# Experts and routing of a four-block network: three orders of work changed

## The chip, the cores and the metric

The kernel runs on one core of one Trainium2 chip. The metric is the device time of one execution in microseconds (us). A core has five engines with instruction streams of their own, which meet only at semaphores: TensorE (matrix products and transposes, called PE in the rows), VectorE (DVE), ScalarE (ACT), GpSimd (POOL) and SyncE (SP), which here only starts transfers and clears semaphores. GpSimd starts the indexed transfers, gathers and scatters.

## The reference, cut to what matters

Four conditioned blocks run one after the other on `x` of 16 x 256 tokens with 256 features. The change lies in the second half of the last one, a mixture of eight experts, each of which chooses its own 512 of the 4096 tokens:

```python
tok = x.reshape(-1, d)                       # 4096 x 256
gate = softmax(tok @ Wgate.T)                # 4096 x 8
vals, idx = jax.lax.top_k(gate.T, k_cap)     # each expert its 512 tokens
g = _ln(tok[idx_flat], mlp_g, mlp_b)         # gathered, normalised
y = gelu(einsum('ked,ehd->keh', g, fc1s) + b1s, approximate=True)
y = einsum('keh,edh->ked', y, fc2s) + b2s
tok = tok.at[idx_flat].add(y * w[..., None]) # scattered back, added
```

## The kernel before, in words

The program is a row of blocks; at the border of a block all engines meet. Attention and MLP blocks fill the first 3126 us. Behind them stand two that the change touches.

`route` (L2465 and on). TensorE turns the 4096 tokens in eight groups of 512 (`transposes`, bank tiles `r_bank`, two sets of two), VectorE evicts the first half `k = 0` of groups 0 to 3 to `r_xt` and ScalarE all other halves; TensorE may write group 2 only when group 0 is evicted on both. Then follow logits, a softmax on VectorE in two halves, a search for each expert's 512th largest gate in 15 rounds of VectorE and TensorE, and the lists of tokens, which become `idx`. VectorE works in the order of the code: constants, a wait for four small loads (`const_in`), four conversions (L2674 to L2677), the evictions (L2681), 14 shifts that fill `r_bits` (L2684), the softmax. At the same time ScalarE rounds the first expert's `moe_w1` to its high part and GpSimd subtracts that from it (L2535), the low part. Last, GpSimd gathers the first expert's tokens in four pieces of 128 into `xg`, all on one semaphore `first_in`.

`experts` (L2807 and on). Each expert has 512 tokens in four tiles (`SC` = 4), features in two halves (`KD` = 2) and a hidden width of 1024 in eight parts (`MC` = 8). Every product is made of three in fp32r with high and low parts (`three`, L2935 to L2937), so every operand is split: ScalarE copies the high part, VectorE subtracts it. In the body of expert e:

- TensorE makes the up products of e, the down products of m = 0 and 1, the transposes of the normalised tokens of e + 1 (`moe_tp`, L2943), and the down products of m = 2 to 7.
- ScalarE makes the gelu and high part of `moe_h` for m = 0 to 7, then the high parts of `moe_xt` and of both weights `moe_w` of e + 1.
- VectorE makes the low parts of `moe_h`; behind m = 2 the statistics of the gathered tokens of e + 1 up to `moe_ve` (`normalise`); behind m = 3 `moe_xn` (`centre`, L2993), for which it needs the root; behind m = 7 `moe_xm` (gain and offset, L3002), the low parts of `moe_xt` and of the up weights; then y (L3032), y2, that is y times the gate (L3038), and the low part of the down weights.
- GpSimd waits for the scatters of e - 1, releases the y2 buffer, makes the reciprocal root `moe_rstd` for e + 1 (`token_rstd`, L2865), copies the indices of the scatter, waits for `moe_xn` of e + 1, gathers the tokens of e + 2, waits for y2 of e and issues its four scatters (L2881).

GpSimd's semaphore waits that other engines' work must not overtake are followed by an increment of their own (`gated_wait`). The root can start when VectorE has written `moe_ve`. Before the loop, the first expert goes through `normalise(0)`, `centre(0)`, `transposes(0)`, `modulate(0)` and `x_hi(0)` as whole steps, each waiting for the whole of the last.

## Time and profile before

| | us |
|---|---|
| median of three runs | 3471.63 |
| lowest, highest | 3470.23, 3478.52 |
| profiled execution | 3478.18 |
| its span, first to last instruction | 3476.4 |
| TensorE busy in the span | 3109.7 (89%) |
| VectorE busy | 2206.5 (63%) |
| ScalarE busy | 1693.4 (49%) |
| GpSimd busy | 807.6 (23%) |
| mean granted clock of TensorE | 0.952 |

Times in the rows are microseconds from the start of the span. A timeline row gives the start, the busy time (of all that are merged in the row, x4 for four), the engine, the line of the kernel, the operation with its result and its sources, and in brackets how long the engine was idle before it and what ended that. The granted clock is TensorE's: 1.00 is 2.4 GHz, 0.50 is 1.2 GHz, and a value between is a mean over the stretch. The ends of matrix products are modelled, so that one reaches beyond the start of the next.

### The profile page before, as it was taken

The page shows a single profiled execution, that of the slowest core. Times are in us where ns is not written, and L with a number is a line of the kernel's source. Part 1 is how long each engine was busy: PE and PEld are TensorE (multiplying, and loading weights), DVE is VectorE, ACT ScalarE, POOL GpSimd, SP SyncE. Part 2 cuts the span into 40 slices and gives each one's busy share as a digit, 9 for nine tenths or more (in the row PEclk, how much of TensorE's full clock was granted, in tenths as well). Part 3 has the DMA queues.
Part 4 walks back from the last instruction along what each step waited for, and adds up shares of the span by engine and source line. Part 5 has one row for each costly group of instructions (what it writes and reads, how often), then busy time and mean ns, then how long its engine had stood idle before and what let it go on. Part 6 is the DMA issues. An engine that isn't in the chain of part 4 may idle for free. (4 is left out here: it accounts for less than half of the span.)

```text
span 3476.4 us, 71011 instructions
## 1 busy us (share of the span) xinstructions
PE 3109.7 (89%) x26346; PEld 2545.5 (73%) x26346; DVE 2206.5 (63%) x4254; ACT 1693.4 (49%) x3084; POOL 807.6 (23%) x656
## 2 busy tenths in 40 slices
PE   7899999997998969999999698799999999982786
PEld 5777877786898959877777587576767676762676
DVE  4566656574666766567777467565656565758564
ACT  3344434443554435545454354565656566651453
POOL 1221112211112321112222111322222222221443
PEclk8999999999999989999999899899999999995898
DMA  4000000000100010100000100000000000003442
GB/s 158 10 6 6 4 5 6 6 6 16 36 19 20 0 46 0 49 1 0 0 0 0 56 24 19 28 1 0 0 0 0 0 0 0 0 14 112 114 114 52
DMA packets 64656, 80.66 MB, mean 23 GB/s; under 512 B 9666, under 2 KB 56514, under 8 KB 64308
## 3 DMA queue, kind: packets, MB, share of 16 engines
q1 hardware_dynamic: 58436, 71.13, 6.7%
q0 software_dynamic: 6144, 8.52, 1.3%
q8 instruction: 46, 0.75, 0.1%
q14 instruction: 30, 0.25, 0.0%
HBM read 66.80 MB, written 12.85 MB: 23 GB/s over the span
## 5 line engine op out<-in xcount | busy, mean ns | idle before, releaser
L915 POOL TENSOR_TENSOR L0a_prob<-L0a_prob 128x1024 f32<-128x1024 f32 x48 | 117.3, 2444 | 570.7 <-PE L0a_o L1270 570.7
L1017 ACT ACTIVATE L0a_prob<-L0a_st 128x512 f32<-128x512 f32 x256 | 138.7, 597 | 201.7 <-PE L0a_st L1237 175.0
L921 POOL TENSOR_TENSOR L3a_shift<-L3a_neg,L3a_mx 128x256 fp32r<-128x256 f32 x128 | 95.7, 748 | 554.5 <-DVE L3a_mx L1496 552.4
L1017 ACT ACTIVATE L3a_prob<-L3a_st 128x512 f32<-128x512 f32 x256 | 138.8, 597 | 128.5 <-PE L3a_st L1237 128.5
L1496 DVE TENSOR_REDUCE L0a_mx<-L0a_s 128x2 f32<-128x512 f32 x256 | 164.4, 683 | 39.2 <-PE L0a_s L1213 37.3
L1845 ACT ACTIVATE L2a_prob<-L2a_st 128x512 f32<-128x512 f32 x256 | 132.2, 604 | 116.3 <-PE L2a_st L1876 116.3
L1486 DVE SCALAR_TENSOR_TENSOR L3a_qk_lo<-raw,cols_sb,L3a_qk_hi 128x256 fp32r<-128x256 f32 x256 | 156.4, 650 | 36.5 <-ACT L3a_qk_hi L1008 36.5
L1496 DVE TENSOR_REDUCE L3a_mx<-L3a_s 128x2 f32<-128x512 f32 x256 | 163.8, 679 | 18.2 <-PE L3a_s L1213 18.1
L2108 DVE TENSOR_REDUCE L2a_mx<-L2a_s 128x2 fp32r<-128x512 f32 x256 | 163.5, 681 | 14.5 <-PE L2a_s L1876 14.5
L1435 DVE RECIPROCAL L0a_rsum<-L0a_sum 128x256 f32<-128x256 f32 x16 | 28.1, 1758 | 197.8 <-PE L0a_sum L1285 176.2
L1435 DVE RECIPROCAL L3a_rsum<-L3a_sum 128x256 f32<-128x256 f32 x16 | 28.1, 1758 | 174.4 <-PE L3a_sum L1285 155.3
L1475 DVE TENSOR_TENSOR L0a_qk_lo<-L0a_st,L0a_qk_hi 128x512 fp32r<-128x512 f32 x128 | 86.8, 687 | 69.9 <-ACT L0a_qk_hi L977 69.8
L915 POOL TENSOR_TENSOR L3a_prob<-L3a_prob 128x1024 f32<-128x1024 f32 x48 | 117.6, 2451 | 52.7 <-PE L3a_o L1270 51.1
L1270 PE MATMUL L3a_o<-L3a_prob,L3a_v 128*64 128x256 f32 x1024 | 124.6, 385 | 0.0
L1270 PE MATMUL L0a_o<-L0a_prob,L0a_v 128*64 128x256 f32 x1024 | 124.6, 385 | 0.0
L972 ACT ACTIVATE L0a_o_hi<-L0a_o 128x512 fp32r<-128x512 f32 x64 | 40.5, 632 | 129.1 <-PE L0a_o L1107 64.7
L1270 PEld LDWEIGHTS L3a_o<-L3a_prob,L3a_v 128*64 128x64 f32 x1024 | 67.8, 136 | 40.8 <-issue 6.6
L1270 PEld LDWEIGHTS L0a_o<-L0a_prob,L0a_v 128*64 128x64 f32 x1024 | 67.8, 136 | 40.7 <-issue 6.6
L990 ACT ACTIVATE L3a_prob<-L3a_st 128x512 f32<-128x512 f32 x128 | 77.2, 603 | 33.9 <-PE L3a_sum L1168 33.9
L1449 DVE TENSOR_TENSOR L3a_o<-raw,L3a_s 128x512 f32<-128x512 f32 x64 | 43.9, 686 | 75.8 <-PE L3a_s L1126 75.8
L1105 PE MATMUL L0a_st<-L0a_xt,L0a_wq 128*128 128x256 f32 x256 | 77.6, 303 | 15.1 <-POOL L0a_wo L909 10.0
L1105 PE MATMUL L3a_st<-L3a_xt,L3a_wq 128*128 128x256 f32 x256 | 77.9, 304 | 11.5 <-POOL L3a_wo L909 8.9
(605 smaller groups left out, 11528.4 us busy)
## 6 DMA issues: line engine op xcount, KB each, us to landing
raw<-in_moe_w SPq DMA_DIRECT2D x16, 1024.0 KB, 6.0
x_sb<-in_x SPq DMA_DIRECT2D x1, 4096.0 KB, 24.5
L0a_gate<-gate_rows SPq DMA_DIRECT2D x32, 128.0 KB, 3.8
L0m_gate<-gate_rows SPq DMA_DIRECT2D x32, 128.0 KB, 3.8
L2a_gates<-gate_rows SPq DMA_DIRECT2D x2, 2048.0 KB, 10.0
L2m_gate<-gate_rows SPq DMA_DIRECT2D x32, 128.0 KB, 3.7
out_x<-x_sb SPq DMA_DIRECT2D x1, 4096.0 KB, 18.0
token_rows<-x_sb SPq DMA_DIRECT2D x1, 4096.0 KB, 29.8
```

The source lines that it names most:

```text
L915: nc.gpsimd.tensor_tensor(both[:, :, :, 0:N], both[:, :, :, 0:N], both[:, :, :, N:2 * N], ALU.add).then_inc(halves_done, 1)
L921: nc.gpsimd.tensor_tensor(shift[:, u % 4, :, :, :], neg64[:].unsqueeze(1).unsqueeze(1).to_broadcast([P, 2, TT, 64]), mx[:, u % 2, :, :].un ...
L990: A(sq[:, c % 4, :], qk_bank(c)[:], ACT.Square).then_inc(sq_done, 1)
L1017: A(prob[:, u % 4, h, :], st_ps[u % 2][h][:], ACT.Exp, scale=64 ** -0.5).then_inc(p_done, 1)
L1105: mm(out, lhs[0], rhs[0], start=start, stop=False, skip_group_check=True)
L1270: last = mm(o_ps[rows(h), (u % 2) * N:(u % 2 + 1) * N], v[:, kt, hd * 64:(hd + 1) * 64], prob[:, u % 4, h, kt * N:(kt + 1) * N], start=(kt ...
L1435: V.reciprocal(rsum[:], sum_ps[:, 0:N]).then_inc(rsum_done, 1)
L1475: V.tensor_tensor(qk_lo[:, c, :], qk_bank(c)[:], qk_hi[:, c, :].bitcast(F32), ALU.subtract).then_inc(qklo_done, 1)
L1486: ins = V.scalar_tensor_tensor(qk_lo[:, u, at], raw[:, u, at], col(name), qk_hi[:, u, at].bitcast(F32), ALU.add, ALU.subtract)
L1496: V.tensor_reduce(mx[:, u % 2, h, :], s_ps[h][:].rearrange("p (t n) -> p t n", t=TT), AX.X, ALU.max).then_inc(mx_done, 1)
L1845: A(prob[:, 2 * (w % 2) + h, :], st_ps[w % 2][h][:], ACT.Exp, scale=0.25).then_inc(p_done, 1)
L2108: V.tensor_reduce(mx[:, w // 2 % 2, :, at], s_ps[h][:].rearrange("p (t n) -> p t n", t=TT), AX.X, ALU.max).then_inc(mx_done, 1)
```

## The change

It has three parts. In the body of each expert GpSimd makes the root of the next expert before it waits for the scatters of the last one, and before it releases y2. In the routing VectorE's wait for the constants and the four conversions stand behind the four evictions and the fourteen shifts. And the first expert is taken by pieces: a semaphore for each of the four gathers; statistics and mean of one tile after the other; `moe_xn` with a signal per tile, behind which TensorE makes that tile's two transposes; `moe_xm` and both parts of `moe_xt` by halves with a signal each. The copies of the gate weights go behind `moe_ve`, and seven more semaphores are in use.

```diff
--- before.py
+++ after.py
@@ -2541,7 +2541,7 @@
             pool.wait_ge(idx_ready, 1)
             for s in range(SC):
                 pool.indirect_dma_start(moe["xg"][:, s, :], None, t["token_rows"][:, :],
-                                        bass.IndirectOffsetOnAxis(ap=g["idx"][:, 0, s:s + 1], axis=0)).then_inc(moe["first_in"], 16)
+                                        bass.IndirectOffsetOnAxis(ap=g["idx"][:, 0, s:s + 1], axis=0)).then_inc(moe["first_in"][s], 16)
 
         @block.scalar
         def _(act):
@@ -2670,11 +2670,6 @@
             V.memset(thr[:], 0).then_inc(ready, 1)
             step(V.tensor_reduce(same[:], g["ident"][:].rearrange("p (t e) -> p e t", e=E), AX.X, ALU.add))
             V.tensor_copy(same_b[:], same[:].unsqueeze(1).to_broadcast([P, HALF, E])).then_inc(ready, 1)
-            dve.wait_ge(const_in, 64)
-            V.tensor_copy(iota_h[:], iota_f[:, 0:LOW]).then_inc(ready, 1)
-            V.tensor_copy(tri_b[:], tri[:]).then_inc(ready, 1)
-            step(V.tensor_scalar(tok_f[:], tval[:], float(P), pval[:, 0:1], ALU.mult, ALU.add))
-            V.tensor_scalar(tok_h[:], tok_f[:], -2048.0, None, ALU.add).then_inc(ready, 1)
             READY = TRIES + 5
             for i in range(4):
                 dve.wait_ge(tp_done, KD * i + 1)
@@ -2682,6 +2677,11 @@
             dve.wait_ge(ready, TRIES + 1)
             for n in range(1, BITS // 2):
                 step(V.tensor_scalar(bits[:, n, :], bits[:, n - 1, :], 2, None, ALU.logical_shift_right))
+            dve.wait_ge(const_in, 64)
+            V.tensor_copy(iota_h[:], iota_f[:, 0:LOW]).then_inc(ready, 1)
+            V.tensor_copy(tri_b[:], tri[:]).then_inc(ready, 1)
+            step(V.tensor_scalar(tok_f[:], tval[:], float(P), pval[:, 0:1], ALU.mult, ALU.add))
+            V.tensor_scalar(tok_h[:], tok_f[:], -2048.0, None, ALU.add).then_inc(ready, 1)
 
             def softmax(h):
                 half = lambda a: a[:, HALF * h:HALF * (h + 1)]
@@ -2828,6 +2828,7 @@
         w1_in, w2_in, b2_in, w1_hi, w1_lo, w2_hi, w2_lo = (sem(x) for x in ("w1_in", "w2_in", "b2_in", "w1_hi", "w1_lo", "w2_hi", "w2_lo"))
         idx_done, gathered, scattered, weight_done, passed, passed_dve = (sem(x) for x in ("idx", "gathered", "scattered", "weight", "passed", "passed_dve"))
         idxo_done, weight_now, y2_free = sem("idxo"), sem("weight_now"), sem("y2_free")
+        first_xn, first_tp, first_xm, first_xhi = (sem(x) for x in ("first_xn", "first_tp", "first_xm", "first_xhi"))
         block = ctx.enter_context(nc.Block())
         w1_d = t["moe_w1"].rearrange("e (k p) n -> e p k n", p=P)
         w2_d = t["moe_w2"].rearrange("e (m p) n -> e p m n", p=P)
@@ -2865,11 +2866,11 @@
                 nc.gpsimd.tensor_tensor(rstd[:], ve[:], g["mhalf"][:, 0:SC], ALU.pow).then_inc(rstd_done, 1)
 
             def body(e, first, more, more2):
+                if more:
+                    token_rstd(e + 1)
                 if not first:
                     gated_wait(scattered, 16 * SC * e)
                 pool.sem_inc(y2_free, 1)
-                if more:
-                    token_rstd(e + 1)
                 nc.gpsimd.tensor_copy(idx_out[:], g["idx"][:, bass.ds(e, 1), :].squeeze(1)).then_inc(idxo_done, 1)
                 gated_wait(idxo_done, e + 1)
                 if more2:
@@ -2920,7 +2921,10 @@
 
             act.sem_inc(w1_hi, 1)
             act.sem_inc(w2_hi, 1)
-            x_hi(0)
+            for k in range(KD):
+                act.wait_ge(first_xm, k + 1)
+                nc.scalar.activation(xt[0][:, k, :], xm[:, k, :], ACT.Copy).then_inc(first_xhi, 1)
+            act.sem_inc(xhi_done, 1)
             body(0, True)
             with act.Fori(1, E - 1) as e:
                 body(e, True)
@@ -2965,7 +2969,13 @@
                         transposes(e + 1)
                 last.then_inc(down_done, 1)
 
-            transposes(0)
+            for s in range(SC):
+                pe.wait_ge(first_xn, s + 1)
+                for k in range(KD):
+                    last = nc.tensor.transpose(tp_ps[k][:, s * P:(s + 1) * P], xn[:, s, k * P:(k + 1) * P], g["ident"][:])
+                    if s == SC - 1:
+                        last.then_inc(first_tp, 1)
+            pe.sem_inc(tp_done, 1)
             with pe.Fori(0, E - 1) as e:
                 body(e, True)
             body(E - 1, False)
@@ -3043,10 +3053,31 @@
                     low(e + 1, w2_hi, w2, stage2, w2_lo)
 
             dve.sem_inc(down_free, 1)
-            normalise(0, moe["first_in"], 16 * SC)
-            centre(0)
-            modulate(0)
+            for s in range(SC):
+                dve.wait_ge(moe["first_in"][s], 16)
+                V.bn_stats(stats[:, s, :], xg[:, s, 0:D]).then_inc(stats_done, 1)
+                dve.wait_ge(stats_done, s + 1)
+                V.bn_aggr(mv[:, s, :], stats[:, s, :]).then_inc(aggr_done, 1)
+            dve.wait_ge(aggr_done, SC)
+            V.tensor_scalar(ve[:], mv[:, :, 1], 1e-5, None, ALU.add).then_inc(ve_done, 1)
+            V.tensor_copy(weight_next[:], xg[:, :, D:D + 1].squeeze(2)).then_inc(weight_done, 1)
             weights_now(0)
+            dve.wait_ge(rstd_done, 1)
+            for s in range(SC):
+                V.tensor_scalar(xn[:, s, :], xg[:, s, 0:D], mv[:, s, 0:1], rstd[:, s:s + 1], ALU.subtract, ALU.mult).then_inc(first_xn, 1)
+            dve.wait_ge(first_xn, SC)
+            dve.sem_inc(xn_done, 1)
+            gain, offset = COL_AT["L3_cond_mlp_g"], COL_AT["L3_cond_mlp_b"]
+            for k in range(KD):
+                dve.wait_ge(first_tp, k + 1)
+                V.tensor_scalar(xm[:, k, :], tp_ps[k][:], g["cols"][:, gain + k:gain + k + 1], g["cols"][:, offset + k:offset + k + 1],
+                                ALU.mult, ALU.add).then_inc(first_xm, 1)
+            dve.wait_ge(first_xm, KD)
+            dve.sem_inc(xm_done, 1)
+            for k in range(KD):
+                dve.wait_ge(first_xhi, k + 1)
+                ins = V.tensor_tensor(xt[1][:, k, :], xm[:, k, :], xt[0][:, k, :].bitcast(F32), ALU.subtract)
+            ins.then_inc(xlo_done, 1)
             low(0, w2_hi, w2, stage2, w2_lo)
             with dve.Fori(0, E - 1) as e:
                 body(e, True)
@@ -3089,7 +3120,7 @@
                "stage2": g["raw"][:, 4:8, :].rearrange("p c (m n) -> p (c m) n", n=D), "w1_in": g["first_w1_in"],
                "w1": [sb(f"moe_w1{j}", [P, KD, MLP], F32R) for j in range(2)],
                "w2": [sb(f"moe_w2{j}", [P, MC, D], F32R) for j in range(2)],
-               "idx_now": sb("moe_idx_now", [P, SC], U32), "xg": sb("moe_xg", [P, SC, ROW]), "first_in": sem("moe_first_in")}
+               "idx_now": sb("moe_idx_now", [P, SC], U32), "xg": sb("moe_xg", [P, SC, ROW]), "first_in": [sem(f"moe_first_in{s}") for s in range(SC)]}
         route(nc, t, g, out, moe)
         experts(nc, t, g, out, moe)
         with nc.Block() as block:
```

The listing of GpSimd's instructions shows the first part. This is the loop over the experts 1 to 5, before; `moe_rstd` is the root, `moe_xg` the gather, `out_x` the scatters, and the rows without a result are arithmetic on registers for the waits.

```order
L2890 ISA
L2852 REGISTER_ALU
L2865 TENSOR_TENSOR moe_rstd<-moe_ve,mhalf 128x4
L2873 ISA
L2873 COPY moe_idx_out<-idx_sb 128x4
L2852 REGISTER_ALU
L2857 ISA
L2857 COPY moe_idx_now<-idx_sb 128x4
L2860 DMA moe_xg<-token_rows,moe_idx_now 128x264 x4
L2881 DMA out_x<-moe_y,moe_idx_out 4096x256 x4
```

The same loop of GpSimd now:

```order
L2891 ISA
L2866 TENSOR_TENSOR moe_rstd<-moe_ve,mhalf 128x4
L2853 REGISTER_ALU
L2874 ISA
L2874 COPY moe_idx_out<-idx_sb 128x4
L2853 REGISTER_ALU
L2858 ISA
L2858 COPY moe_idx_now<-idx_sb 128x4
L2861 DMA moe_xg<-token_rows,moe_idx_now 128x264 x4
L2882 DMA out_x<-moe_y,moe_idx_out 4096x256 x4
```

The root stands first, before the register for the scatters' count is made; everything behind has its old order. The second part, on VectorE at the start of the routing, `-` before and `+` now:

```order
 L2671 TENSOR_REDUCE r_same<-ident_sb 128x8
 L2672 CAST r_same_b<-r_same 128x128
-L2674 CAST r_iota_h<-r_iota_f 128x32
-L2675 CAST r_tri_b<-r_tri 128x128
-L2676 TENSOR_SCALAR r_tok_f<-r_tval,r_pval 128x32
-L2677 TENSOR_SCALAR r_tok_h<-r_tok_f 128x32
-L2681 COPY r_xt<-r_bank 128x512 x4
-L2684 TENSOR_SCALAR r_bits<-r_bits 128x3 x14
+L2676 COPY r_xt<-r_bank 128x512 x4
+L2679 TENSOR_SCALAR r_bits<-r_bits 128x3 x14
```

The four evictions and the fourteen shifts are ahead of the four conversions, which follow there and are followed by the softmax as before.

## Rows read from the trace of the kernel before

**Rows 1.** Waits of GpSimd and TensorE, 2990 to 3480: total, times, longest us.
```profile
POOL moe_rstd L2865 <- DMA out_x<-moe_y,moe_idx_out: 20.6, 6, 3.6
...
PE moe_tp L2943 <- DVE moe_xn L2993: 22.8, 7, 9.2
```

**Rows 2.** Timeline of GpSimd, expert 1: start, us, operation, idle before.
```profile
3274.11 1.04 POOL L2865 TENSOR_TENSOR moe_rstd<-moe_ve,mhalf 128x4 f32<-128x4 f32 x1 [3.29 <-DMA out_x<-moe_y,moe_idx_out]
```

**Rows 3.** Timeline of VectorE, experts 0 to 6.
```profile
3258.74 1.42 DVE L3032 TENSOR_TENSOR moe_y<-moe_down,moe_b 128x256 f32<-128x256 f32 x4 [1.82 <-PE moe_down L2937]
...
3268.35 0.17 DVE L2988 TENSOR_SCALAR moe_ve<-moe_mv 128x4 f32<-128x4 f32 x1
...
3275.19 1.38 DVE L2993 TENSOR_SCALAR moe_xn<-moe_xg,moe_mv,moe_rstd 128x256 f32<-128x256 f32 x4 [6.04 <-POOL moe_rstd L2865]
...
3287.26 1.41 DVE L3032 TENSOR_TENSOR moe_y<-moe_down,moe_b 128x256 f32<-128x256 f32 x4
...
3432.58 1.42 DVE L3032 TENSOR_TENSOR moe_y<-moe_down,moe_b 128x256 f32<-128x256 f32 x4 [0.55 <-PE moe_down L2937]
```

**Rows 4.** Timeline of TensorE, experts 1 to 3.
```profile
3277.47 0.36 PE L2935 MATMUL moe_down<-moe_w,moe_h 128*128 128x256 f32 x1
...
3285.92 0.28 PE L2937 MATMUL moe_down<-moe_w,moe_h 128*128 128x256 f32 x1
...
3287.39 0.50 PE L2935 MATMUL moe_up<-moe_xt,moe_w 128*128 128x512 f32 x1 [1.19 <-DVE moe_w L3010]
...
3305.14 1.09 PE L2943 MATMUL moe_tp<-ident_sb,moe_xn 128*128 128x128 f32 x8 [2.06 <-DVE moe_xn L2993]
...
3316.08 0.40 PE L2935 MATMUL moe_up<-moe_xt,moe_w 128*128 128x512 f32 x1
```

**Rows 5.** Stretches: busy us of each engine, granted clock, DMA share, GB/s.
```profile
3272.00:3276.00 4.00, 2.57 (x22) 2.36 (x21) 0.81 (x3) 0.00 (x0) 1.20 (x2) 1.00 0.31 48
3306.00:3310.00 4.00, 4.00 (x24) 4.00 (x22) 2.48 (x5) 2.39 (x4) 2.83 (x3) 0.57 0.12 34
```

**Rows 6.** Timelines in the routing: GpSimd, ScalarE, VectorE, TensorE.
```profile
3128.68 4.48 POOL L2535 TENSOR_TENSOR moe_w<-raw,moe_w 128x2048 fp32r<-128x2048 f32 x1
...
3128.32 1.06 ACT L2553 ACTIVATE r_xt<-r_bank 128x512 f32<-128x512 f32 x2
...
3129.81 3.39 DVE L2674 CAST r_iota_h<-r_iota_f 128x32 f16<-128x32 f32 x1 [1.92 <-DMA r_tri<-in_tri]
...
3133.61 1.28 DVE L2681 COPY r_xt<-r_bank 128x512 f32<-128x512 f32 x2
...
3137.81 2.81 DVE L2684 TENSOR_SCALAR r_bits<-r_bits 128x3 uint32<-128x3 uint32 x14
...
3142.78 0.29 DVE L2690 COPY r_logit<-r_bank 128x128 f32<-128x128 f32 x1 [2.15 <-PE r_bank L2604]
...
3134.35 5.01 PE L2584 MATMUL r_bank<-ident_sb,x_sb 128*128 128x128 f32 x24 [5.88 <-DVE r_xt L2681]
...
3139.29 1.06 PE L2574 MATMUL r_bank<-r_xt,r_wide_wg 128*32 128x512 f32 x8
```

**Rows 7.** Timelines of GpSimd and VectorE, two earlier places.
```profile
46.52 2.50 POOL L900 TENSOR_TENSOR L0a_wv<-L0a_prob,L0a_wv 128x1024 fp32r<-128x1024 f32 x1 [8.30 <-ACT L0a_wv L1083]
...
47.81 1.25 DVE L1409 TENSOR_SCALAR L0a_ve<-L0a_mv 128x2 f32<-128x2 f32 x1
...
1085.61 0.98 POOL L386 TENSOR_TENSOR L1a_rstd<-L1a_ve,mhalf 128x2 f32<-128x2 f32 x1 [4.00 <-DVE L1a_ve L593]
...
1085.94 0.42 DVE L691 COPY L1a_v_row<-L1a_pt_ps 128x256 f32<-128x256 f32 x1
```

**Rows 8.** Timelines of VectorE and TensorE, first expert.
```profile
3221.59 0.17 DVE L2980 COPY moe_weight_next<-moe_xg 128x4 f32<-128x4 f32 x1 [4.31 <-PEq L2465]
...
3228.32 1.53 DVE L3002 TENSOR_SCALAR moe_xm<-moe_tp,cols_sb 128x512 f32<-128x512 f32 x2 [2.06 <-PE moe_tp L2943]
...
3232.34 0.76 PE L2935 MATMUL moe_up<-moe_xt,moe_w 128*128 128x512 f32 x1 [4.06 <-DVE moe_xt L3006]
```

## The prediction

> **What bounds the kernel now.** I read the waits first, over the last 486 us (the end of the attention, the routing and the experts), since everything that the diff touches lies there. Two rows stand out [rows 1]: GpSimd's reciprocal root `moe_rstd` waited 20.6 us in six waits for the scatters into `out_x` to land, and TensorE's transposes `moe_tp` waited 22.8 us in seven waits for VectorE's `moe_xn`, which needs that root. The six are the bodies of experts 1 to 6.
>
> The timelines of expert 1's body show one loop. GpSimd's root starts at 3274.11, after 3.29 us of waiting for the landing, so the last of the four scatters was issued by 3270.82 [rows 2]. VectorE had the root's input `moe_ve` at 3268.52, then sat idle 6.04 us until `moe_xn` at 3275.19 [rows 3]. From y to y an expert takes 28.52 us here (3258.74 to 3287.26), and (3432.58 - 3258.74) / 6 = 28.97 us on the mean of experts 0 to 6 [rows 3]. TensorE is full otherwise but not the only bound: it waits 2.06 us before the transposes of the next expert, and 1.19 us at 3287.39 for the low half of `moe_w` [rows 4], because the work behind the root (last `moe_h`, `moe_xm`, `moe_xt`, `moe_w`) came late as well. And in expert 2 the granted clock was 0.57 from 3306 to 3310 while in the same part of expert 1, 3272 to 3276, it was 1.00 [rows 5]: it fell behind the idle pieces of two experts in a row.
>
> In the routing, the chain is: transposes, evictions, logits, softmax on VectorE. VectorE's first conversion, 32 elements a row, took 3.39 us, from 3129.81 to 3133.20; GpSimd's subtraction for `moe_w` ran from 3128.68 to 3133.16. The first two evictions start behind it at 3133.61 and TensorE's third group of transposes waits 5.88 us for them [rows 6].
>
> **A: the root ahead of the wait for scatters.** Nothing is added or taken out; GpSimd's 1.04 us root moves ahead of a wait. It is queued behind the four scatter issues still, so it starts at 3270.8 plus 0.3 us, my estimate of the hand-over from the issue to the root: 3271.1 in place of 3274.1, a shift of 3.0 us. Its input is there since 3268.5. What is late next:
> - The chain through the root. From y to root: 3271.15 - 3258.74 = 12.4 us. From root to the next y: 3287.26 - 3274.11 = 13.15 us, unchanged, as all of it is serial behind the root on VectorE and ScalarE. Sum 25.5 us.
> - TensorE. From the first up product at 3287.39 to the transposes at 3305.14, less the 2.06 us, 15.7 us; transposes 0.9 of their 1.09, the rest being the drain; the rest of the down products at the full clock, 3277.47 to 3285.92 and one pitch of 0.12, 8.6 us [rows 4]. Sum 25.2 us, just under the chain's 25.5.
> So the period goes from 28.97 to 25.5 us, six times: 173.84 - 153.2 = **20.6 us**. It is more than six times 3.0 because the longer experts also lose their stretch at the low clock and their slower landings. What was moved past: the scatter wait now stands ahead of the index copies, the release of `y2` and the next gather. The gather's place was behind `moe_xn` anyway; the landing (3273.8, 0.3 before the old root) comes 0.2 us after the new end of `moe_xn` (3273.6), so the gather too starts almost 3 us earlier, and it is wanted only in the next expert. Low end for A: only TensorE's own wait goes, 6 x 2.06 = 12.4. High end: a period of TensorE's 25.2, 22.6.
>
> **B: conversions behind the first evictions.** In the new order VectorE goes to the evictions right after `same_b`. ScalarE's first eviction starts at 3128.32, two take 1.06 [rows 6], so the first is done at 3128.95, and TensorE's third group can start at 3129.0 in place of 3134.35. Three groups of 8 at the pitch of the full clock take some 2.9 us in place of 5.0, so the logits start at 3131.9 in place of 3139.29, and the softmax, 3.49 us behind them (3142.78 - 3139.29), could start at 3135.4. VectorE itself is later: evictions done at about 3131.2, then 14 shifts of `bits` (2.81 us [rows 6]), then four conversions (0.6 us without the stall). If the shifts are free of GpSimd's subtraction they end at 3134.0 and the conversions at 3134.6: softmax at 3135.4, 7.4 us gained. If they wait for its end at 3133.16, as the conversion did, the softmax starts at 3136.6: 6.1 gained. Here is what the rows give: a scalar operation of 2 elements, SBUF to SBUF, started at 47.81 beside GpSimd's product of 46.52 and took 1.25 us, where `moe_ve` of 4 elements takes 0.17 [rows 3], to 49.06, the product's end 49.02; a copy of 256 elements out of PSUM beside GpSimd's root at 1085.61 took its plain 0.42 [rows 7]. The shifts are of the first sort, the evictions of the second, so I take **6.1 us**. The searches behind are one chain and only move; GpSimd's first gather moves with its index; the row store's last wait was over long before. The low end is 0.4: the evictions stall too and start at 3133.2 in place of 3133.61.
>
> The Trainium skill, SBUF — State Buffer, "Who interferes with whom", says that a single-source VectorE operation within SBUF in a two-port mode and a GpSimd operation exclude each other for the whole instruction, and one with a PSUM source does not take part. The rows 6 and 7 agree to 0.04 us. By that rule the evictions are free and the shifts are held, which is the 6.1; without the rule for shifts it would be 7.4.
>
> **C: the first expert by pieces.** VectorE starts at 3221.59, and what it stood idle for in front of that was the block's border (PEq), not a gather [rows 8]: they have landed. So waiting per gather brings nothing. Statistics and means taken in turn cost four waits between them in place of one: some +0.3 us. Then `moe_xn` in four with a signal each: before, all 1.38 us of it [rows 3] came first and then all eight transposes, for which VectorE stood idle 2.06 us until 3228.32 [rows 8]; now TensorE starts behind the first quarter, 1.0 us earlier, less the 0.3. Then, before, both `moe_xm` (1.53), ScalarE's half, VectorE's half and the up products at 3232.34, 4.0 us behind 3228.32 [rows 8]. In halves: the first `moe_xm` starts one transpose (2.06 / 8, 0.26 us) before the last ends and takes 0.8, the second follows, ScalarE's halves lie beside it, VectorE's second half ends 0.6 after ScalarE's second: some 2.8 us. Sum -0.3 + 1.0 + 1.2 = **2.0 us** nearly exactly (3230.3 in place of 3232.3). Bounds: 0 (the semaphores eat it) to 2.5. The seven new semaphores are cleared at the end, 0.1 us or so: left out.
>
> **Sum.** 20.6 + 6.1 + 2.0 = 28.7 us off the profiled execution's own 3478.18 (span 3476.4): 3449.5. That execution was 6.55 above the median of the three runs, 3471.63; off the median it is 3442.9, which is the forecast.
>
> **Rivals.**
> - *The clock keeps falling.* For it: expert 2 had the fall, by the mean of 28.97 against expert 1's 28.52 others had it too (I take experts 2, 4 and 6), and TensorE still has short waits for `moe_h` in each expert. Against: the two longest idle pieces (2.06 and 1.19) go. Then every second expert has its transposes and the rest of its down products slow as now (3305.14 to 3316.08, 10.9 in place of 9.5 [rows 4]) and a period of 15.7 + 10.9 = 26.6: A is 173.84 - 3 x 25.53 - 3 x 26.6 = 17.4, sum 25.5, 3446.1. The Trainium skill, TensorE: Matmul & The Clock Gate, Part 1, has the clock released by activity and throttled after idleness; that speaks for the forecast, rows 5 agree with the direction.
> - *The evictions stall beside GpSimd.* B is 0.4, sum 23.0, 3448.6. Rows 7's copy out of PSUM is against it.
> - *Something else takes the root's place.* GpSimd is in line again with gather and scatters, or a transfer of weights arrives late since the loads, scatters and gathers now come closer; then only TensorE's own wait is saved: 12.4 + 6.1 + 2.0 = 20.5, 3451.1. For it: loads, gathers and scatters of an expert share 29 us today and 25.5 then. Against: no transfer holds anyone in rows 1 but the scatters that root.
> - *Slower.* The tighter loop leaves TensorE at 1.2 GHz through whole experts, as it was in the routing. An expert's up and down products are some 22 us at the full clock (13 or more of the 15.7, and the 8.6) and as much again at half; from 28.7 us of work done at half the clock, 1.3 experts, the change costs time. At two and a half: 3471.6 + 55 - 28.7 = 3498. Nothing in rows 5 has the clock fall while TensorE is full; it is here because all of A leans on the clock.
> - *It doesn't do what it says:* no, the order of GpSimd's row changes in the loop as the listing shows.
>
> **Chances.** Forecast 0.62 (its own range 3439 to 3447), clock 0.13, evictions 0.08, other bound 0.12, no visible change 0.03, slower 0.02. The range 3437 to 3457 takes in A's and B's ends but one (both lows together, 3458). About 0.3%, 10.4 us, can be told from no change: every case but the last two saves 20 us or more, so faster 0.95, same 0.03, slower 0.02.
>
> **What would show it.** A: root starts 0.3 us behind the last scatter issue, no wait for landings in front of it; y to y near 25.5 for experts 1 to 6; transposes wait under 0.3 us; clock 1.00 from 3240 on. B: third group of transposes some 2.5 us behind the first, shifts beside GpSimd's subtraction with the first stretched to its end, softmax 6 us sooner after the routing's start. C: up products 8.7 us behind the block's border in place of 10.8. It is wrong if a period stays above 27 us, or if the routing (its start to the first gather) is less than 4 us shorter.

## The result, and the profile after

The changed kernel takes 3439.34 us in the median of five runs (3433.54 to 3446.91), the kernel before 3471.63 in the median of five beside them (3463.62 to 3478.52): a ratio of 0.9905, 95% interval 0.9891 to 0.9919. The forecast was 3442.9 us (range 3437 to 3457), on the side of faster with 0.95.

The profiled execution took 3443.93 us with a span of 3442.1, against a span of 3476.4 before. Of these 34.3 us, 4.4 are no part of the change: the routing starts at 3122.18 where before it started at 3126.56, and nothing in front of it was touched. From the routing's start to the end the changed kernel takes 319.9 us and the kernel before 349.8: **29.9 us less, where the sum of the prediction was 28.7**. Split at rows that both traces have (us; `r_gate_t` VectorE's copy of the transposed gates, "border" is VectorE's first row of the experts, "up" TensorE's first up product, y0 to y7 VectorE's `moe_y` of the eight experts):

| stretch | before | after | only A | only B | only C |
|---|---|---|---|---|---|
| routing's start to `r_gate_t` | 29.46 | 23.19 | 29.44 | 23.15 | 29.48 |
| `r_gate_t` to border | 65.57 | 65.62 | 65.63 | 65.65 | 65.55 |
| border to up | 10.75 | 9.07 | 10.75 | 10.74 | 9.08 |
| up to y0 | 26.40 | 25.75 | 26.26 | 26.12 | 25.60 |
| y0 to y6 (six experts) | 173.84 | 152.36 | 151.66 | 174.25 | 174.45 |
| y6 to y7 | 23.50 | 23.53 | 23.49 | 23.52 | 23.50 |

So B is 6.3 us, C 1.7 (up to the first up product), A 21.5. Another 0.65 us lie between up and y0, in the first expert; whether C made them is taken up below.

The waits of the changed kernel from y0 to y6 (total, times, longest us), for [rows 1]:

```profile
DVE moe_xn L3003 <- POOL moe_rstd L2866: 16.8, 6, 2.8
...
POOL moe_idx_out L2874 <- DMA out_x<-moe_y,moe_idx_out: 13.6, 6, 2.5
...
PE moe_up L2939 <- ACT moe_h L2910: 6.8, 12, 1.1
```

The wait for the landing has gone over to `moe_idx_out`, behind the root, and harms nobody. The row in which the transposes waited for `moe_xn` is gone from the middle experts. One expert's body on GpSimd (start, us, operation, idle before), for [rows 2]:

```profile
3325.54 3.05 POOL L2882 DMA_INDIRECT out_x<-moe_y,moe_idx_out  x1 [6.52 <-DVE moe_y L3048]
3328.90 1.56 POOL L2882 DMA_INDIRECT out_x<-moe_y,moe_idx_out  x1 [0.30 <-issue]
3330.76 1.55 POOL L2882 DMA_INDIRECT out_x<-moe_y,moe_idx_out  x1 [0.30 <-issue]
3332.62 1.55 POOL L2882 DMA_INDIRECT out_x<-moe_y,moe_idx_out  x1 [0.30 <-issue]
3333.62 1.63 POOL L2866 TENSOR_TENSOR moe_rstd<-moe_ve,mhalf 128x4 f32<-128x4 f32 x1
3337.43 0.49 POOL L2874 COPY moe_idx_out<-idx_sb 128x4 uint32 x1 [2.17 <-DMA out_x<-moe_y,moe_idx_out]
```

and on VectorE, for [rows 3]:

```profile
3322.11 1.41 DVE L3042 TENSOR_TENSOR moe_y<-moe_down,moe_b 128x256 f32<-128x256 f32 x4
...
3324.81 2.29 DVE L3020 TENSOR_TENSOR moe_w<-raw,moe_w 128x2048 fp32r<-128x2048 f32 x1
...
3335.29 1.38 DVE L3003 TENSOR_SCALAR moe_xn<-moe_xg,moe_mv,moe_rstd 128x256 f32<-128x256 f32 x4 [2.78 <-POOL moe_rstd L2866]
...
3347.44 1.41 DVE L3042 TENSOR_TENSOR moe_y<-moe_down,moe_b 128x256 f32<-128x256 f32 x4
```

The root stands right behind the fourth issue; its row even overlaps it, and less the overlap (to 3334.17) it is 1.08 us. `moe_xn` follows it at once, and y comes 25.33 us behind y. TensorE in the same expert (the first row after each of its waits), for [rows 4]:

```profile
3322.25 0.50 PE L2939 MATMUL moe_up<-moe_xt,moe_w 128*128 128x512 f32 x1 [0.44 <-DVE moe_w L3020]
...
3328.63 0.50 PE L2939 MATMUL moe_up<-moe_xt,moe_w 128*128 128x512 f32 x1 [0.63 <-ACT moe_h L2910]
...
3333.44 0.50 PE L2939 MATMUL moe_up<-moe_xt,moe_w 128*128 128x512 f32 x1 [0.43 <-ACT moe_h L2910]
```

Its idle time is down to 1.5 us an expert. One whole expert as a stretch (busy us of TensorE, its weight loads, VectorE, ScalarE and GpSimd with their instructions, granted clock, DMA share, GB/s), for [rows 5]:

```profile
3322.20:3347.50 25.30, 23.98 (x152) 21.10 (x152) 18.14 (x37) 14.89 (x20) 13.51 (x11) 1.00 0.49 130
```

The granted clock is 1.00 in every one of the middle experts. In the routing, GpSimd, VectorE and TensorE, for [rows 6]:

```profile
3124.29 4.55 POOL L2535 TENSOR_TENSOR moe_w<-raw,moe_w 128x2048 fp32r<-128x2048 f32 x1
...
3122.18 0.12 DVE L2669 MEMSET r_bits<- 128x1 uint32 x3 [0.36 <-PEq L758]
...
3132.15 0.28 DVE L2690 COPY r_logit<-r_bank 128x128 f32<-128x128 f32 x1
...
3145.37 0.42 DVE L2712 COPY r_gate_t<-r_bank 128x256 f32<-128x256 f32 x1 [0.57 <-PE r_bank L2618]
...
3124.66 2.91 PE L2584 MATMUL r_bank<-ident_sb,x_sb 128*128 128x128 f32 x24 [0.58 <-ACT r_xt L2553]
...
3126.20 0.69 DVE L2676 COPY r_xt<-r_bank 128x512 f32<-128x512 f32 x1 [0.18 <-PE r_bank L2584]
```

The third group of transposes starts 2.5 us behind the first and waits only 0.58 us, for ScalarE's eviction, where it waited 5.88. VectorE's eviction takes 0.69 us beside GpSimd's subtraction. The 24 transposes of that row take 2.91 us at a granted clock of 1.00, where before they took 5.01 at 0.55; the softmax starts 10.0 us after the routing's start in place of 16.2. In the first expert, for [rows 8]:

```profile
3210.99 0.43 DVE L3058 BATCH_NORM_STATS2 moe_stats<-moe_xg 128x6 f32<-128x256 f32 x1 [2.19 <-PEq L2465]
...
3216.95 1.53 DVE L3073 TENSOR_SCALAR moe_xm<-moe_tp,cols_sb 128x512 f32<-128x512 f32 x2 [0.88 <-PE moe_tp L2975]
...
3220.06 0.76 PE L2939 MATMUL moe_up<-moe_xt,moe_w 128*128 128x512 f32 x1 [2.94 <-DVE moe_xt L3079]
```

### The profile page after: what moved, and what is told of

It is laid out like the page before. It is cut to its first block and busy times, and to the rows that moved or that the text cites. A ratio compares the mean times of both kernels' runs of the same rounds, so it can differ in the third digit from the quotient of the medians.

```text
span 3442.1 us, 71017 instructions
## 1 busy us (share of the span) xinstructions
PE 3093.8 (90%) x26346; PEld 2530.8 (74%) x26346; DVE 2204.7 (64%) x4255; ACT 1694.4 (49%) x3085; POOL 804.7 (23%) x656
```

## The experiments

**Each part alone.** The three kernels are the one before with one part of the diff each.

Only A:
```
-                if not first:
-                    gated_wait(scattered, 16 * SC * e)
-                pool.sem_inc(y2_free, 1)
                 if more:
                     token_rstd(e + 1)
+                if not first:
+                    gated_wait(scattered, 16 * SC * e)
+                pool.sem_inc(y2_free, 1)
```


> The kernel before, with part A alone: GpSimd's root of the next expert stands ahead of its wait for the scatters to land. Theory (the parts stand apart, and A carries three quarters of the gain): from y to y 25.4 us in the six middle experts as with all three parts, where before had 28.97, so 6 x 3.6 = 21.5 us less, 3450.1 us against 3471.6; the stretch from the routing's start to the first up products stays as before. Rival (A needs B or C, because the TensorE clock falls again where the experts start later, or the gathers then come late): the period stays at 26 us or more, and the time is 3454 us or more. Rival (A is less than its share and B and C hold the rest): 3460 us.

Measured: 3452.31 us, ratio 0.9937 (0.9923 to 0.9952). Six middle experts take 151.66 us, 25.28 each, and the stretches ahead of them are those of before (table). The theory holds, and no rival: A stands by itself.

Only B:
```
-            dve.wait_ge(const_in, 64)
-            V.tensor_copy(iota_h[:], iota_f[:, 0:LOW]).then_inc(ready, 1)
...
             for n in range(1, BITS // 2):
                 step(V.tensor_scalar(bits[:, n, :], bits[:, n - 1, :], 2, None, ALU.logical_shift_right))
+            dve.wait_ge(const_in, 64)
+            V.tensor_copy(iota_h[:], iota_f[:, 0:LOW]).then_inc(ready, 1)
...
```


> The kernel before, with part B alone: the routing's conversions stand behind VectorE's four evictions and the shifts. Theory: the softmax starts 10.0 us after the routing's start instead of 16.2, and the copy of the transposed gates comes 6.3 us sooner after it; everything behind it keeps its length, so 3465.3 us against 3471.6 (ratio 0.9982). Rival (a later wait eats the gain, the store of the gates or the weights' load): the first gather starts less than 6 us sooner, and the time stays within 0.05% of the kernel before.

Measured: 3465.92 us, ratio 0.9978 (0.997 to 0.9987). `r_gate_t` comes 6.3 us sooner after the routing's start, and the stretch behind it is as long as before, 65.65 us: nothing later eats it.

Only C:
```
-            normalise(0, moe["first_in"], 16 * SC)
-            centre(0)
-            modulate(0)
+            for s in range(SC):
+                dve.wait_ge(moe["first_in"][s], 16)
+                V.bn_stats(stats[:, s, :], xg[:, s, 0:D]).then_inc(stats_done, 1)
...
```


> The kernel before, with part C alone: the first expert's normalisation, transposes, modulation and parts in pieces. Theory: the first up products start 9.1 us after the block's border instead of 10.75, and the clock rises 2.6 us earlier in them, which gives 0.65 us more up to the first y: together 2.3 us, 3469.3 us against 3471.6, a ratio of 0.9993 that a timing alone hardly shows. Rival (the gathers land one by one too late for pieces to help without the earlier routing): 10.5 us or more from border to up products, no change in time.

Measured: 3471.76 us, ratio 0.9997 (0.9988 to 1.0006): no difference that timing can show. The trace shows border to up 9.08 us in place of 10.75, and up to y0 25.60 in place of 26.40. Up to the first y the trace has 2.5 us less, of which the 1.7 up to the up products are C's own; whether the rest is, stays open (below). The 2.3 us forecast are neither confirmed nor refuted by the times. The three ratios add to 0.9912, the whole has 0.9905.

**GpSimd's subtraction out of the shifts' time.** The changed kernel with this:
```
+            pool.wait_ge(stored, 48)
             pool.wait_ge(w1_hi, 1)
             nc.gpsimd.tensor_tensor(moe["w1"][1][:], moe["stage1"][:], ...)
```
(The wait and the subtraction go from their old place behind the waits for `made`, `shifts_made` and `wide_made`.)


> The changed kernel, with GpSimd's subtraction for the low part of w1 (4.55 us, 128x2048) moved from the routing's start to behind the landing of the gates' store, out of the time of VectorE's shifts. Theory (the first of the 14 shifts stands until GpSimd's subtraction ends): the shifts take 2.8 us instead of 4.7, the softmax then waits for TensorE's logits, which are there 8.7 us after the routing's start, so its first copy comes at 8.7 instead of 10.0: 1.3 us less, and the subtraction in its new place beside the search of thresholds holds up one of VectorE's operations there or none: the time is between 1.3 us less and 3 us more than that of the changed kernel. Rival (the shifts are slow for a reason of their own, such as following the evictions): they take 4.7 us again and the softmax starts 10.0 us after the routing's start.

In the changed kernel the shifts beside the subtraction (its row is above) were

```profile
3126.81 4.72 DVE L2679 TENSOR_SCALAR r_bits<-r_bits 128x3 uint32<-128x3 uint32 x14
```

and in this one, with the subtraction elsewhere (VectorE, then GpSimd, then VectorE):

```profile
3126.16 2.80 DVE L2679 TENSOR_SCALAR r_bits<-r_bits 128x3 uint32<-128x3 uint32 x14
...
3130.28 0.29 DVE L2690 COPY r_logit<-r_bank 128x128 f32<-128x128 f32 x1 [0.61 <-PE r_bank L2604]
...
3156.88 4.49 POOL L2539 TENSOR_TENSOR moe_w<-raw,moe_w 128x2048 fp32r<-128x2048 f32 x1 [33.20 <-DMA token_rows<-r_gates]
...
3155.11 0.16 DVE L2717 TENSOR_TENSOR r_cand<-r_tried,r_delta 128x3 uint32<-128x3 uint32 x1
...
3157.17 0.15 DVE L2728 TENSOR_SCALAR r_delta<-r_passes 128x1 uint32<-128x1 f32 x1
3157.36 4.04 DVE L2717 TENSOR_TENSOR r_cand<-r_tried,r_delta 128x3 uint32<-128x3 uint32 x1
```

The shifts are free, the softmax now waits for TensorE, and `r_gate_t` comes 21.98 us after the start in place of 23.19. But an operation on 3 elements that takes 0.16 us took 4.04 beside the subtraction, to 3161.40, its end being 3161.37. `r_gate_t` to border is 69.51 us, 3.9 more. The sum is 2.7 us lost in the trace, inside the expected range of 1.3 less to 3 more. The median was 3446.33 us, 7 above the changed kernel's and outside that range; but the ratio, 0.9924 (0.991 to 0.9938), is not surely apart from the 0.9905 of the changed kernel. That an operation of VectorE can be held to the end of GpSimd's subtraction is shown twice, and where the subtraction stands in the changed kernel it costs 1.2 us, less than here.

**The root later by about a microsecond.** The changed kernel with a fill ahead of every root:
```
                 gated_wait(ve_done, e + 1)
+                nc.gpsimd.memset(pad[:], 0.0).then_inc(pad_done, 1)
+                gated_wait(pad_done, e + 1)
                 nc.gpsimd.tensor_tensor(rstd[:], ve[:], ...)
```


> The changed kernel, with a fill of 128x1024 elements on GpSimd, and a wait for it, ahead of each root: by the fills of the routing (0.53 us for 128x512) it makes the root 1.1 to 1.2 us later. Theory (in the six middle experts the chain from y over the scatters' issue, the root, xn and VectorE's parts of h to the next w sets the period): y to y goes from 25.4 to 26.5 us, 7 us more in six experts, about 3446.5 us. Rival (TensorE, busy 23.9 of 25.4 us, sets the period, and the root has slack): 25.4 to 25.7 us, 3440 to 3441.5 us.

GpSimd, one body:

```profile
3341.72 1.54 POOL L2867 MEMSET moe_pad<- 128x1024 f32 x1
3343.45 1.04 POOL L2869 TENSOR_TENSOR moe_rstd<-moe_ve,mhalf 128x4 f32<-128x4 f32 x1 [0.18 <-POOL moe_pad L2867]
```

With y at 3330.24 the root ends 14.25 us behind y, in the changed kernel 13.14 (3335.25 - 3322.11): 1.11 later. Six experts take 159.10 us in place of 152.36, 1.12 us each: one for one. The time is 3453.24 us, ratio 0.9935 (0.992 to 0.995), clearly slower than the changed kernel, and above my 3446.5: outside the six experts the trace has 1.7 us more (1.1 for the first expert's own root, 0.6 between up and y0), and the rest of the distance between the medians is not explained. The chain through the root sets the period of the changed kernel.

**The root earlier.** The changed kernel with the root between the second and the third scatter:
```
                 for s in range(SC):
+                    if s == 2 and more2:
+                        token_rstd(e + 2)
                     pool.indirect_dma_start(out.rearrange(...), ..., y2[:, s, :], ...)
```


> The changed kernel, with the root put between the second and the third scatter of the expert before, so that two scatters are issued ahead of it instead of four. It then waits for ve, which is there 9.7 us after y; it ends 11.4 us after y instead of 13.1. Theory (chain over the root sets the period): xn comes 1.7 us sooner, TensorE's wait of 0.5 us at the start of each expert goes and its own work is next: y to y 24.9 us instead of 25.4, 3 us less in six experts, about 3436.5 us. Rival (TensorE sets the period already): 25.4, no change. Rival (third and fourth scatter, 1.7 us later, delay the gathers of the expert after next until VectorE's statistics wait for them): 25.4 or more, with a wait for the gather at VectorE.

GpSimd, VectorE, TensorE in one body:

```profile
3330.95 1.55 POOL L2884 DMA_INDIRECT out_x<-moe_y,moe_idx_out  x1 [0.30 <-issue]
3334.14 1.34 POOL L2866 TENSOR_TENSOR moe_rstd<-moe_ve,mhalf 128x4 f32<-128x4 f32 x1 [1.64 <-DVE moe_ve L3000]
3335.69 1.71 POOL L2884 DMA_INDIRECT out_x<-moe_y,moe_idx_out  x1 [0.21 <-issue]
...
3324.05 1.42 DVE L3044 TENSOR_TENSOR moe_y<-moe_down,moe_b 128x256 f32<-128x256 f32 x4 [1.54 <-PE moe_down L2943]
...
3330.70 0.50 PE L2941 MATMUL moe_up<-moe_xt,moe_w 128*128 128x512 f32 x1 [1.19 <-ACT moe_h L2912]
```

The root ends 11.43 us behind y, 1.7 sooner, as meant; y now waits 1.54 us for TensorE. Yet six experts take 151.79 us, 25.30 each, 0.1 less than before the edit. The time is 3444.34 us, ratio 0.991 (0.9895 to 0.9925). My 24.9 was wrong and the rival nearly right: right behind the chain through the root, at most 0.1 us away, stands another. (The rival gave TensorE's own work as the reason, and that was wrong too: TensorE still waits for `moe_h`.) TensorE's wait at the expert's start went, but the 0.63 us for the third `moe_h` became 1.19: VectorE's subtraction for `moe_w` behind y stands ahead of the first two parts of h, and holds back with them ScalarE and TensorE. The run with both moves, below, bears this out: with the subtraction gone from there, that wait is 0.27 us.

**The subtraction for w2 later.** The changed kernel with it behind the fourth part of h, where VectorE waits for the root (the call ahead of the loop goes too):
```
+                    if m == 3:
+                        low(e, w2_hi, w2, stage2, w2_lo)
...
-                    low(e + 1, w2_hi, w2, stage2, w2_lo)
```


> The changed kernel, with VectorE's subtraction for the low part of w2 (2.29 us, 128x2048) moved from the start of the expert, where the first scatter's issue runs beside it and takes 3.05 us instead of 1.55, to behind the fourth part of h, where VectorE waits 2.8 us for the root. Theory (the subtraction holds the issue up): the first issue takes 1.55 us, the root starts 1.5 us sooner, xn follows the subtraction, 0.5 us sooner than now, and TensorE's wait for the third gelu, 0.6 us, goes: y to y 24.9 us, 3 us less in all, about 3436.5 us. Rival (the root, an operation of GpSimd on the same port, is now held up until the subtraction ends): the root's row is stretched to over 3 us, xn is 1 us later, y to y 26.4 us, 3445 us. Rival (the first issue is long for another reason): it takes 3.05 us again, the root stands where it is, xn follows at the same time, 25.4 us.

GpSimd, then VectorE, in one body (y at 3326.98):

```profile
3330.41 2.07 POOL L2882 DMA_INDIRECT out_x<-moe_y,moe_idx_out  x1 [2.52 <-DVE moe_y L3050]
...
3336.51 3.37 POOL L2882 DMA_INDIRECT out_x<-moe_y,moe_idx_out  x1 [0.30 <-issue]
3339.34 1.63 POOL L2866 TENSOR_TENSOR moe_rstd<-moe_ve,mhalf 128x4 f32<-128x4 f32 x1
...
3330.30 0.69 DVE L3030 TENSOR_TENSOR moe_h<-moe_h 128x512 fp32r<-128x512 f32 x1 [0.53 <-ACT moe_h L2913]
...
3336.17 2.28 DVE L3020 TENSOR_TENSOR moe_w<-raw,moe_w 128x2048 fp32r<-128x2048 f32 x1
```

It got slower than the changed kernel in the trace: 157.01 us for six experts, 26.17 each, where I had expected 24.9; the time is 3447.22 us, ratio 0.9922 (0.9909 to 0.9936), which timing alone can't tell from the changed kernel's 0.9905. The subtraction holds an issue up in either place: the first issue is now short, 2.07 us, but the fourth takes 3.37, and the root ends 14.0 us behind y. It was not the root that was held, as the rival had it, but the issue ahead of it.

**Both moves.** The root between the scatters and the subtraction behind the fourth part of h.


> The changed kernel with both: the root between second and third scatter, and the subtraction for w2 behind the fourth part of h. Theory: the root is ready 2 us before xn needs it, xn starts behind the subtraction, 1.5 us sooner than now; then TensorE sets the period with 23.9 us of its own and what is left of its waits: y to y 24.3 us, 6.5 us less than the changed kernel, about 3433 us. Rival (root and subtraction hold each other up): 25.4 us or more, no gain.

VectorE, the fifth of the six periods (the first y of them stands at 3246.57, the fifth at 3342.20):

```profile
3342.20 1.42 DVE L3046 TENSOR_TENSOR moe_y<-moe_down,moe_b 128x256 f32<-128x256 f32 x4 [0.50 <-PE moe_down L2943]
...
3352.95 0.17 DVE L2992 COPY moe_weight_next<-moe_xg 128x4 f32 x1 [4.46 <-DMA moe_xg<-token_rows,moe_idx_now]
...
3372.49 1.42 DVE L3046 TENSOR_TENSOR moe_y<-moe_down,moe_b 128x256 f32<-128x256 f32 x4 [1.83 <-PE moe_down L2943]
```

3431.73 us (3430.86 to 3440.57), ratio 0.9876 (0.9861 to 0.9891). The first four periods are 23.9 us on the mean, better than my 24.3, and the sixth is 23.8; the fifth is 30.3. In it VectorE waits 4.5 us for a gather, TensorE 4.8 us in its turn for `moe_h`, and behind that wait the granted clock is 0.51 from 3354 to 3360, where it was 1.00 in the periods before: the wait for the gather is 4.5 us of the 6.4 that the period is longer, and the other two go with the slow clock. The other three runs took 3430.86 to 3431.86 us, so by their times they had no such period. Two moves of which one gave 0.1 us an expert and one cost 0.8 give 1.5 together: each had run into the limit that the other takes away.

**The gathers ahead of the landing wait**, on top of both moves:
```
+                if more2:
+                    gated_wait(xn_done, e + 2)
+                    gated_wait(weight_done, e + 2)
+                    gather(e + 2)
                 if not first:
                     gated_wait(scattered, 16 * SC * e)
```
(The same four lines go from their place behind the copy of the indices.)

> The kernel of the two moves, with GpSimd's gathers of the expert after next ahead of its wait for the scatters to land. In the two moves' run five of six middle periods took 23.8 to 24.1 us and one 30.3, in which VectorE waited 4.5 us for a gather whose issues ended 4.6 us after y. Theory (those gathers are late since they stand behind the landing of the late scatters): here they are issued from the end of xn on, 5 us sooner, no period is long, y to y 23.85 us in all six, and the time is at the fastest of the two moves' runs, about 3431 us. Rival (the long period comes from the DMA queues being full with the next weights, whatever the issue): a period of 27 us or more again, and the same spread of times. Rival (the earlier issues now stand beside VectorE's subtractions and push the scatters or the root back): y to y over 24.3 us.

VectorE's y of experts 0 and 6, and one stretch:

```profile
3244.46 1.42 DVE L3046 TENSOR_TENSOR moe_y<-moe_down,moe_b 128x256 f32<-128x256 f32 x4 [0.69 <-PE moe_down L2943]
...
3387.22 1.42 DVE L3046 TENSOR_TENSOR moe_y<-moe_down,moe_b 128x256 f32<-128x256 f32 x4 [0.47 <-PE moe_down L2943]
```

```profile
3275.00:3300.00 25.00, 24.75 (x159) 22.10 (x158) 19.77 (x44) 16.24 (x22) 16.53 (x12) 1.00 0.56 156
```

3431.33 us (3430.49 to 3431.89), ratio 0.9884 (0.9866 to 0.9902). All six periods are 23.8 us, y waits for TensorE in each, TensorE is busy 24.75 of 25 us, and the four runs lie within 1.4 us. The trace agrees with the theory. It does not settle it: only one of the four runs with the two moves had the long period, so four runs without one could be chance, and whether the late issue or a slow landing made that gather late is open. By time this kernel (0.9884) and the one with the two moves (0.9876) can't be told apart, and its interval overlaps the changed kernel's (0.9891 to 0.9919). What it gains on the changed kernel is read in the trace, 9.6 us in the six experts (152.36 - 142.76).

## Why the prediction was right

- **A, 20.6 forecast, 21.5 measured.** The chain y, scatters' issue, root, y was put at 12.4 + 13.15 = 25.5 us; it is 25.4. The hand-over of 0.3 us behind the last issue doesn't show: the root ends 1.08 us after the issue's end, its own time being 1.04. The late root shows that this chain bounds, one for one. So this step was right in its mechanism.
- **TensorE's 25.2 us "just under".** As a number it came out (25.3 with the root out of the way), and that was luck; as a name it was wrong. The 15.7 us from the first up product to the transposes held two waits for `moe_h`, 1.06 us together, which I counted as work (kernel before, expert 2):

```profile
3293.78 0.50 PE L2935 MATMUL moe_up<-moe_xt,moe_w 128*128 128x512 f32 x1 [0.63 <-ACT moe_h L2909]
...
3298.58 0.50 PE L2935 MATMUL moe_up<-moe_xt,moe_w 128*128 128x512 f32 x1 [0.43 <-ACT moe_h L2909]
```

  With the subtraction moved as well an expert takes 23.8 us, and that is TensorE. So the 22.6 that I gave as the high end of A was the next chain, not an engine at its limit: with that chain cut as well, the six experts lose 31.1 us (173.84 - 142.76).
- **The clock.** Before, it was 0.94 on the mean of experts 2, 4 and 6 (29.1 to 29.3 us each) and 1.00 in 1, 3 and 5 (28.5 to 28.9), as the prediction took it. It is 1.00 in all six now; the rival that had it fall in every second one is out. In only B and only C the periods stay uneven and at 29.0 to 29.1 us on the mean.
- **B, 6.1 forecast, 6.3 measured.** Evictions out of PSUM, TensorE's result memory, ran free beside GpSimd's subtraction (0.69 us each), the shifts were held to its end (4.72 us in place of 2.81). The held shifts cost 1.2 us against TensorE's logits: the 7.4 of the other case would be 7.5.
- **C, 2.0 forecast, 1.7 measured to the up products**: the statistics with four waits end 0.4 us later in place of 0.3, the rest gave 2.1 in place of 2.2. (These terms add to 1.9, not to the 2.0 that the prediction wrote.) What I had left out is the clock: in the changed kernel and in only C TensorE was at full clock earlier in the up products (below), and up to y0 they take 0.65 and 0.8 us less than the kernel before. Whether that is C's doing is open. Seven of the kernels with C take 25.3 to 25.8 us there, the three without it 26.1 to 26.4. But the kernel with the late root, which has all of C, has the clock at 0.50 until five us after its first up product and takes 26.33 us, of which its later root may be a part.
- **Something else takes the root's place.** No transfer did. In the middle experts no engine waited for a gather in this kernel (VectorE waited 0.39 us for one in the first expert); with both moves one such wait came up.
- **Median.** 3442.9 forecast, 3439.34 measured. The trace has 1.2 us more than the sum. The other 2.4 are not explained and lie within the scatter: the five runs differ by 13 us, and the routing, with nothing changed ahead of it, starts anywhere from 3121.1 to 3128.6 us in the traces of this case. That the medians came so close is in part luck.
- **A slip in the range.** Both low ends together are 12.4 + 0.4 + 2.0 = 14.8 us, 3456.8, which is inside the range and not the 3458 beyond it.

The stretches of the first up products (columns as above), in the changed kernel, whose first up product starts at 3220.06:

```profile
3218.00:3222.00 4.00, 1.94 (x5) 1.58 (x6) 3.85 (x4) 2.33 (x3) 3.39 (x3) 0.50 0.25 68
3222.00:3224.00 2.00, 2.00 (x8) 1.60 (x7) 0.12 (x1) 0.97 (x2) 1.70 (x2) 0.72 0.28 68
```

and in the kernel before, where it starts at 3232.34:

```profile
3236.00:3238.00 2.00, 2.00 (x7) 1.57 (x6) 0.69 (x1) 0.79 (x2) 0.00 (x0) 0.54 0.92 278
3238.00:3240.00 2.00, 2.00 (x10) 1.63 (x9) 0.69 (x1) 1.84 (x3) 0.00 (x0) 1.00 0.57 198
```

Two to four us after the start the mean is between the levels of 1.2 and 2.4 GHz in the one, four to six us after in the other. The runs don't show why.

## To carry to other kernels

An engine takes its instructions in order, so a wait delays everything behind it: look which later instruction does not need what is waited for, and put it ahead. The next limit may stand 0.1 us behind the one removed, as here, and one edit at a time then shows nothing or a loss; read which wait grew (here 0.63 to 1.19 us) and make both edits. And when a stretch of TensorE is added up as its own work, take the waits inside it off first.

## What the runs showed of the hardware

**A VectorE subtraction with both inputs in SBUF (the core's working memory) holds up the issue of an indirect DMA by GpSimd that begins during it.** A scatter's issue then ends 1.4 to 1.5 us after the subtraction's end, about its own time of 1.55: 3328.59 against 3327.10 in the changed kernel (3.05 us long), 3339.88 against 3338.45 (3.37) and 3332.48 against 3330.99 (2.07) with w2 later. In the traces of before, after, late root, early root, w2 later and the last two kernels, 109 issues begin at least 0.4 us before the end of one such f32 subtraction (for `moe_h`, `moe_w` or `moe_xt`). 106 of them last, within 0.2 us, what is left of it plus their own 1.55 us (scatter) or 0.95 (gather). Scatters' issues begun outside take 1.55 us, also where a short subtraction starts while they run (3328.90 to 3330.46 beside the one from 3329.28). A second subtraction right behind the first did not make it longer (two for `moe_h` from 3327.01 on, in the changed kernel). The worst case is the routing's first gather: 10.63 us beside a row of fp16 operations back to back, where the next took 0.96:

```profile
3194.23 10.63 POOL L2543 DMA_INDIRECT moe_xg<-token_rows,idx_sb  x1 [65.38 <-DVE idx_sb L2779]
3205.16 0.96 POOL L2543 DMA_INDIRECT moe_xg<-token_rows,idx_sb  x1 [0.30 <-issue]
...
3195.93 7.81 DVE L2763 TENSOR_TENSOR r_onehot<-r_iota_h,r_low_h 128x1024 f16<-128x1024 f16 x4
```

It ends 1.1 us after the last of them (3203.74). Here the hold did last over the whole row; the runs don't show what makes the difference.

The Trainium skill, SBUF — State Buffer, "Who interferes with whom", says that a probe saw a `tensor_copy` stall a DMA and a `tensor_tensor` not, and infers as the reason that descriptor generation needs only the part of the shared ports that `tensor_tensor` leaves alone. The rows above differ from that, and the measurement decides. The same section has a two-input VectorE operation contend with a GpSimd instruction that reads SBUF; whether the issue, whose indices lie there, is held as such a reader, no run here shows.

**What is held in the other direction** goes with where the operands lie, in the rows of this case: beside GpSimd's 4.5 us subtraction, evictions out of PSUM ran at 0.69 us, while operations on 3 elements within SBUF, of one input (the shifts) and of two (`r_cand`, 4.04 us in place of 0.16), waited for its end. One exception shows that this is not all: the operation on a single element within SBUF at 3157.17 took its 0.15 us beside the same subtraction.
